# Another rhythm of waits in the scatter of edges, and another engine for half of the float8 target tables, in a four-layer graph network on Trainium2

## The reference

```python
f0 = segment_sum(x[src], dst)
f1: out = relu(relu(((1 + eps) * x + segment_sum(relu(x[src] + edge_attr), dst)) @ W1.T + b1) @ W2.T + b2)
f2 = segment_sum(x[dst] * edge_weight, src) @ weight
f3: deg = segment_sum(1, src); norm = deg**-0.5 at src times the same at dst
    gate = sigmoid(x[src] @ w_src + x[dst] @ w_tgt + bias); f3 = segment_sum(norm * gate * x[src], dst)
```

## Time and profile before

| | |
|---|---|
| runs | 11771.89, 11788.64, 11806.3 us |
| the profiled execution | 11785.09 us |
| its span, first to last instruction | 11783.3 us |
| busy, share of the span | TensorE matmul 53%, weight load 47%, VectorE 58%, ScalarE 34%, GpSimd 27% |
| mean granted clock of TensorE | 0.715 |
| DMA | 1319.70 MB, mean 112 GB/s |
| GpSimd L659 | 3224 scatters, 3134.0 us busy |
| ScalarE L1338 | 728 casts, 1187.9 us busy |
| VectorE L953 | 728 writes, 466.7 us busy |

### The profile page before, as it was taken

The page is one execution under the profiler, slowest core; times in us unless marked ns, Lnnn a source line. Parts: engine busy times, 40 slices in busy tenths (PEclk is TensorE's granted clock), DMA queues, the critical chain, the costliest instruction groups (busy, mean ns, idle before and its releaser), DMA issues.

```text
span 11783.3 us, 289152 instructions
## 1 busy us (share of the span) xinstructions
PE 6214.0 (53%) x120824; PEld 5502.5 (47%) x120824; DVE 6783.5 (58%) x8443; ACT 4037.9 (34%) x6116; POOL 3179.5 (27%) x3346
## 2 busy tenths in 40 slices
PE   2222222222222222249995666666666667688886
PEld 2111111111111111138884665666666666588886
DVE  3222222222222222259987888886777777888885
ACT  1000000000000000025544555554888888233321
POOL 5666666666666666630000000000000000000000
PEclk6555555555555555579997888886666666799997
DMA  8931111111111111125544555553555555355552
GB/s 152 168 56 22 22 22 22 22 22 22 22 22 22 22 22 22 22 91 171 170 143 153 191 193 192 190 192 122 188 183 186 186 183 184 126 168 170 167 168 81
DMA packets 1123617, 1319.70 MB, mean 112 GB/s; under 512 B 581317, under 2 KB 869253, under 8 KB 1122183
## 3 DMA queue, kind: packets, MB, share of 16 engines
q1 hardware_dynamic: 716445, 572.55, 19.0%
q10 hardware_dynamic: 302952, 675.90, 17.0%
q0 software_dynamic: 103168, 54.68, 2.2%
HBM read 902.26 MB, written 400.43 MB: 111 GB/s over the span
## 4 chain that ended last, share of the span: by engine, by line
issue 24%; DVE 19%; another core or an unknown queue 18%; ACT 17%; PE 12%; ACTq 4%; DMA 3%; DVEq 2%; SPq 0%
ACT far_now L1338 9%; DVE hot_d L935 9%; ACT near_now L1301 4%; PE banks L1442 4%; DMA source_marks<-near_now 3%; DVE hot_t L945 2%; PE banks L1532 2%; DVE left L1083 2%; DVE msg_z L1091 2%; ACT msg_z L1330 1%; PE banks L1425 1%; PE banks L1467 1%; PE banks L1435 1%; ACTq L1341 1%
## 5 line engine op out<-in xcount | busy, mean ns | idle before, releaser
L659 POOL DMA_INDIRECT slot_table<-recs,idx_now x3224 | 3134.0, 972 | 981.3 <-issue 967.1
L1442 PE MATMUL banks<-moved,hot_r 128*128 128x196 bf16 x3224 | 726.8, 327 | 2528.0 <-issue 2393.7
L788 DVE TENSOR_TENSOR moved<-hot_h,banks 128x6076 bf16<-128x6076 bf16 x52 | 172.7, 3320 | 3133.1 <-remote 1744.0
L1532 PE MATMUL banks<-hot_d,msg 128*96 128x256 bf16 x10192 | 1469.2, 296 | 555.7 <-DVE msg L1012 458.8
L1442 PEld LDWEIGHTS banks<-moved,hot_r 128*128 128x128 bf16 x3224 | 362.7, 118 | 2864.1 <-issue 2707.2
L1532 PEld LDWEIGHTS banks<-hot_d,msg 128*96 128x96 bf16 x10192 | 1202.6, 131 | 675.2 <-DVE msg L1012 418.0
L935 DVE TENSOR_TENSOR hot_d<-lodl,banks 128x2560 bf16<-128x2560 bf16 (+1 forms) x884 | 1486.6, 1682 | 3.9 <-remote 3.2
L1338 ACT CAST far_now<-hot_td 128x1792 fp8e4<-128x1792 bf16 x728 | 1187.9, 1679 | 34.6 <-DVE hot_td L953 33.2
L1199 ACT CAST lodl<-banks 128x196 f32 (+1 forms) x52 | 16.8, 323 | 3442.9 <-remote 1952.0
L1586 PE MATMUL banks<-x_win,hot_td 128*128 128x32 bf16 x30576 | 880.6, 184 | 206.9 <-issue 190.6
L1586 PEld LDWEIGHTS banks<-x_win,hot_td 128*128 128x128 bf16 x30576 | 837.9, 101 | 222.8 <-issue 207.7
(11 more groups left out here) (187 smaller groups left out, 10653.3 us busy)
## 6 DMA issues: line engine op xcount, KB each, us to landing
lo_bc<-row_table ACTq DMA_DIRECT2D x364, 448.0 KB
dl_bc<-row_table SPq DMA_DIRECT2D x364, 448.0 KB, 4.3
target_marks<-far_now ACTq DMA_DIRECT2D x364, 448.0 KB, 3.6
dl_bc<-target_marks SPq DMA_DIRECT2D x364, 448.0 KB, 4.1
lo_bc<-row_table ACTq DMA_DIRECT2D x468, 320.0 KB
slot_table<-zeros SPq DMA_DIRECT2D x52, 1617.0 KB, 10.7
rec_in<-slot_table ACTq DMA_DIRECT2D x364, 231.0 KB, 2.7
source_marks<-near_now ACTq DMA_DIRECT2D x364, 224.0 KB, 2.3
```

Source lines behind the costliest of these rows:

```text
L659: pool.indirect_dma_start(out=slot_dram[c.number], out_offset=bass.IndirectOffsetOnAxis(ap=idx_now[:, c.slot, g:g + 1], axis=0), in_=recs[ ...
L1442: mm = t.matmul(banks[:, 5, 0:2 * HB].rearrange("p (q h) -> p q h", q=2), group_of(hot_r, g), moved[:, :, g // 2, :, g % 2], start=(g == 0 ...
L1532: mm = t.matmul(banks[0:3 * D, 6 + blk.par, 0:WIN], rows[:, blk.slot, g, :], hot[:, blk.slot, g // 2, :, g % 2], start=(blk.b == 0 and g = ...
```

## The change

The semaphore of the scatters becomes one for each slot. GpSimd waits after the scatters 16, 32 and 48 of a chunk for all scatters of that slot issued until then, the last one among them, and waits for nothing of the other slot; `spent` is raised at the same three places. The other waits on `scattered` are the same in effect.

In layer 2 `hot_td` keeps the lower half alone, in bf16. VectorE writes the upper half as float8 straight into `far_now` (through the view `far8`), and before this second write it waits until the DMA out of this slot of `far_now` has landed. ScalarE casts only the lower half. TensorE takes its weights for k = 1 from `far_now`.

```diff
-RUN = 8
-RUNS = (32, 30)
+RUN = 16
...
-        hot_td = sb("hot_td", [P, 2, 2, BG * P], BF16, late)
+        hot_td = sb("hot_td", [P, 2, BG * P], BF16, late)
...
+        far8 = far_now[:, :, :].bitcast(F8).rearrange("p s (k m) -> p s k m", k=2)
...
-        scattered = [[sem(f"scattered{s}_{odd}") for odd in (0, 1)] for s in (0, 1)]
+        scattered = [sem(f"scattered{s}") for s in (0, 1)]
...
                     elif c.turn:
-                        wait_scattered(sp, c.slot, c.turn)
+                        sp.wait_ge(scattered[c.slot], 16 * G * c.turn)
...
-                        in_=recs[:, c.slot, g, :], in_offset=None).then_inc(scattered[c.slot][g // RUN % 2], 16)
-                    if g == RUN - 1 and c.number:
-                        wait_scattered(pool, 1 - c.slot, (c.number + 1) // 2)
-                    elif g % RUN == RUN - 1 and g > RUN:
-                        odd, run = (g // RUN - 1) % 2, (g // RUN - 1) // 2
-                        pool.wait_ge(scattered[c.slot][odd], 16 * (RUNS[odd] * c.turn + RUN * (run + 1)))
-                    if g + 1 in (24, 40, 56):
+                        in_=recs[:, c.slot, g, :], in_offset=None).then_inc(scattered[c.slot], 16)
+                    if g % RUN == RUN - 1:
+                        pool.wait_ge(scattered[c.slot], 16 * (G * c.turn + g + 1))
+                    if g + 1 in (16, 32, 48):
                         pool.sem_inc(spent, 1)
...
-                dve.wait_ge(far_kept, 2 * blk.number + 2)
-                for k in (0, 1):
-                    v.tensor_scalar(hot_td[:, blk.slot, k, :], dl_bc[:, blk.across], part_col[:, 1 + k:2 + k], None,
-                                    ALU.is_equal).then_inc(hot_t_made[q], 1)
+                dve.wait_ge(far_kept, blk.number + 1)
+                v.tensor_scalar(hot_td[:, blk.slot, :], dl_bc[:, blk.across], part_col[:, 1:2], None, ALU.is_equal
+                                ).then_inc(hot_t_made[q], 1)
+                dve.wait_ge(far_out[blk.slot], 16 * blk.per_chunk * blk.turn + 16 * (blk.place // 2) + 16)
+                dve.sem_inc(passed, 1)
+                v.tensor_scalar(far8[:, blk.slot, 1, :], dl_bc[:, blk.across], part_col[:, 2:3], None, ALU.is_equal,
+                                saturate=False).then_inc(hot_t_made[q], 1)
...
-            act.sem_inc(far_kept, 4)
+            act.sem_inc(far_kept, 2)
...
-                    for k in (0, 1):
-                        s.copy(far_now[:, blk.slot, k * (BG * P // 2):(k + 1) * (BG * P // 2)].bitcast(F8),
-                               hot_td[:, blk.slot, k, :], saturate=False).then_inc(far_kept, 1)
-                    act.wait_ge(far_kept, 2 * blk.number + 6)
+                    s.copy(far8[:, blk.slot, 0, :], hot_td[:, blk.slot, :], saturate=False).then_inc(far_kept, 1)
+                    act.wait_ge(far_kept, blk.number + 3)
...
-                                mm = t.matmul(banks[:, 7, D * g:D * g + D], hot_td[:, blk.slot, k, slots_of(blk, g)],
-                                              x_win[:, blk.par, k, q * D:(q + 1) * D], start=(k == 0 and q == 0),
+                                hot = far8[:, blk.slot, 1, slots_of(blk, g)] if k else hot_td[:, blk.slot, slots_of(blk, g)]
+                                mm = t.matmul(banks[:, 7, D * g:D * g + D], hot, x_win[:, blk.par, k, q * D:(q + 1) * D], start=(k == 0 and q == 0),
                                               stop=(k == 1 and q == 2))
```

More of the change, by code:

```diff
@@ L344, in tables_zeroed @@
             return 16 + 16 * min(BATCH * (j + 1), NCH - 2)
-        def wait_scattered(eng, slot, times):
-            for odd in (0, 1):
-                eng.wait_ge(scattered[slot][odd], 16 * RUNS[odd] * times)
         def wait_alone(eng, semaphore, value):
@@ L672, in _ @@
             for slot in (0, 1):
-                wait_scattered(pool, slot, TURNS)
+                pool.wait_ge(scattered[slot], 16 * G * TURNS)
             def fast():
@@ L1291, in load @@
                     if blk.b == 0:
-                        wait_scattered(act, blk.par, blk.turn + 1)
+                        act.wait_ge(scattered[blk.par], 16 * G * blk.turn + 16 * G)
                     load_rec(blk)
```

## The result

The changed kernel takes **12039.19 us** (four runs, 12032.53 to 12063.82) against 11780.26 us for the kernel before beside it (four runs, 11766.26 to 11806.3); the ratio is 1.0226, interval 1.0214 to 1.0238. The forecast was 12010, in a range of 11860 to 12200.

What follows compares the result with a forecast made beforehand. ScalarE was taken to set layer 2's period, and VectorE's late release, not GpSimd, the scatter chunk's length. 11785 + 177 (layer 2) + 45 (scatter stage) = 12007, against the median 12010 us; range 11860 to 12200.

Steps and rivals of the forecast that it cites:

- the term of layer 2: Layer 2: VectorE's second write waits for a DMA landing, 5.27 us a block against 4.74; +177 us over 338 blocks.
- the scatter stage: Sorting and scattering edges, 700 to 5080 us: the added GpSimd waits cost +45 us, all in the first six chunks.
- B: Layer 2 rival: float8 write goes one element at a time, 2.03 us; 5.74 us a block, total 12170; chance 0.10.
- C: Layer 2 rival: float8 write no slower, 0.68 us; 5.07 us a block, +110, total 11945; chance 0.08.
- The loop of two blocks: Layer 2: `left`, ScalarE's casts, DMA issue to landing, VectorE's second write, back to `left`; 10.54 us for two blocks.
- the turns of the loop: Layer 2: 26 blocks at loop turns, where a 5 us TensorE pause lets the DMA land; no added time.
- The price of a pause: Scatter stage: each added GpSimd wait for a landing costs 0.95 to 1.25 us, 3.3 us a chunk.
- the steady state: Scatter stage after the first six chunks: VectorE's release stays where it is, so the pauses cost 0.
- rival D: Scatter stage: pauses free VectorE, GpSimd becomes the bound, 15 us less in each of 45 chunks; total 11335; chance 0.09.
- 98 us a chunk as before: Scatter stage sign: chunk length stays 98 us despite three gaps between scatters in each chunk.
- Rival A: Scatter stage: VectorE's release (let-go) moves with GpSimd's end, so every chunk pays the pauses; +150, total 12160; chance 0.13.
- Rival E: Layer 2: landings of 2.5 to 2.7 us, 4.62 to 4.72 us a block; no change, 11790 to 11825; chance 0.05.

Runs made afterwards that it cites:

- four slots: The changed kernel with four slots of `far_now` in place of two, each reused after three or four blocks; 11712.43 us against 11796.85 for the kernel before, ratio 0.9937.

## Why the prediction was right, point by point

The sign and the range held, and the total came out 29 us off. That it is so near is partly luck: the term of layer 2 was 118 us too small and that of the scatter stage, read from the profile, 65 us too large, so that the two errors cancel by half.

- **The part of layer 2: right in kind, 118 us too small** (+177 forecast, +295 in the profile). That the landing ends VectorE's second wait, that `left` and ScalarE close a loop over two blocks with it, and that ScalarE falls idle is all there. The float8 write lasts 1.152 us, 1.095 was taken; rivals B (2.03) and C (0.68) fall. VectorE's own period is 4.34 us (4.46 forecast). The Trainium skill, "VectorE: DVE Perf Modes", on the 4x mode, by which a float8 write would not stay at 0.68 us, agrees with the 1.152. Two steps were off. The loop of two blocks was put at 10.54 us with one landing of 3.8; the landings are of two kinds, and most pairs are 4.34 + 6.8 = 11.1 us. Over all blocks that are no turns the mean distance of two far DMAs is 5.43 against 4.78 us, x337 = +219, where +177 was taken. The second, and the larger error, was the turns of the loop, "I leave them as they are", with a pause of 5 us in which the DMA would land. The turn blocks take 12.3 us against 9.3 on average, x26 = +78, where nothing was taken. VectorE does wait for the landing there, 2.4 to 4.1 us in 23 of the 25 turns after the first, but in most turns this wait lies inside TensorE's first gap with nothing shown and does not come on top of it. One turn, VectorE and TensorE:

```profile
8417.31 1.15 DVE L948 TENSOR_SCALAR far_now<-dl_bc,part_col 128x1792 fp8e4<-128x1792 bf16 x1 [2.86 <-DMA target_marks<-far_now]
```

```profile
8420.05 0.26 PE L1580 MATMUL banks<-x_win,hot_td 128*128 128x32 bf16 x3 [5.78 <-issue]
8424.19 0.26 PE L1580 MATMUL banks<-x_win,far_now 128*128 128x32 bf16 x3 [3.24 <-issue]
```

  What grows is those gaps themselves: 9.0 us a turn at the median against 7.1 before. With four slots, where no landing is waited for, they are 8.2 us and the turn blocks 11.7 on average, so most of the turns' growth is not the landing. Why the gaps are longer is open.
- **The Trainium skill, "DMA: Bandwidth & Descriptors", anatomy of one DMA,** gave 3.05 us for 448 KB as an estimate. Its fit is for DMAs issued from GpSimd, and this one is issued from ScalarE. The far DMA lands in 2.5 us when it is alone, which is better than that, and in 4.5 to 5.5 on average where a labels' load leaves in the 2 us ahead of it; the loss hangs on the second kind.
- **The scatter stage: +45 forecast, -20 in the profile** and about -115 in other executions. The price of a pause was underrated (1.65 us; 0.95 to 1.25 forecast), and in the first chunks it is 10 to 12 us for the first two pauses, not 6.7; the first six chunks take 53 us more, where 45 was taken. That would have made the stage slower than forecast. The step that failed is the steady state: "three pauses of a microsecond are little against that" set rival D aside. A pause does free TensorE, by a half: VectorE is let go inside every second chunk. Rival D gave it 0.09 and a GpSimd-bound 83 us a chunk; with three pauses it is met for nine chunks only, with seven for the whole stage. The first chunks' long gaps, which I only counted as a price, let the ranking run eight chunks ahead, and this paid them back. The sign "98 us a chunk as before" came true only on the mean of a pair: 85 and 112.
- **Rival A,** the let-go moving with the end of the scatters, falls: it comes in the midst of them. **Rival E,** landings at the short end, holds for every second block and so for neither.
- The last chunk's let-go after 23 us, the row on which rival D rested, fits with this: something other than the scatters' end can free VectorE. What frees it there is still open.

What stays open: why TensorE creeps while GpSimd scatters on the chips of most runs and not on two, whether GpSimd's issuing or the traffic of its DMAs holds TensorE up, whether the length of a run or the time without scatters counts, and what chooses between the two groups of the three-pause rhythm. Not tried: the changed kernel on a chip without the hold-up; by the pauses' price it should lose there in both parts, which is an estimate.

## What to carry to other kernels

A write moved from an engine that waits late to one that waits early takes the buffer's wait with it: count the loop from the landing of one DMA to the issue of the next, and buy a slot before moving the work. A landing in such a loop is not its median but a distribution, which here depends on whether another large load was issued in the 2 us ahead of it. An engine that stands with nothing shown as releaser, in steps of a fixed length, may be held up by a neighbour: try breaking the neighbour's run before counting the pause as pure cost, and measure on more than one chip.

## What the runs showed that was not expected

- TensorE is slow while GpSimd issues indirect DMAs back to back, on some chips: from some 12 us of them on, matmuls start 0.7 us or a multiple apart. Breaking the run of scatters every eighth time (1.65 us each), from the seventh chunk on, is worth 1503 us of 11749.
- The kernel before takes 11749 to 11797 us on some chips and 8223 and 8235 us on two others. No trace of it was taken there, but those of the kernels with pauses show the same from layer 2 on: with five pauses 1844.8 us between first and last cast, against 1853.2 before, and 3604.5 us from the first cast to the end, against 3607.4. So the difference lies ahead of layer 2, in the scatters and in layers 0 and 1, which there run beside them.
- One rhythm of pauses has two groups of times, some 95 us apart, on one chip.
